# Summing chunks in four column quarters, and adding parts and base weights by matmuls, in a conditioned adapter kernel

## The chip, the cores and the metric

One core of a Trainium2 chip. The metric is the device time of one execution in microseconds (us), the median of the runs shown. Engines: TensorE (PE; PEld is its weight load), VectorE (DVE), ScalarE (ACT), GpSimd (POOL), SyncE (SP, which issues all transfers here).

## The reference

```
B, L, D, N, H = 4, 1024, 512, 128, 128
dWd = ((h @ Wdd.T + bdd) * 0.1).reshape(B, N, D)     # Wdd is (N*D, H): 32 MB
dWu = ((h @ Wdu.T + bdu) * 0.1).reshape(B, D, N)     # Wdu is (D*N, H): 32 MB
down = relu(einsum('bld,bnd->bln', x, Wd + dWd) + bd)
up   = einsum('bln,bdn->bld', down, Wu + dWu) + bu
return x + up                                        # x is (4, 1024, 512)
```

All is fp32. h is the condition, one row of 128 for each of the four batches. Four rows of h meet 131,072 rows of Wdd and Wdu, so that the work is mostly to read these two tensors and to turn their H axis onto the partitions.

## The kernel before, in words

Wdd and Wdu are read in 32 chunks each of 1 MB: a chunk is 2,048 rows, 16 on each of 128 partitions, in a ring of four buffers `w`. For each chunk VectorE transposes 32 x 32 blocks (L240, two instructions for the halves of H, `wt_front_ready` and `wt_ready`) from `w` into a ring of four buffers `wt`. H then lies in four quarters r, with 32 values of H and four row blocks q on the partitions.

TensorE sums a chunk (`sum_chunk`, L414): for each r one fp32 matmul with 512 moving columns of `wt`. The stationary operand `st` holds the values of h, placed so that chunk s of a group of four writes its own 16 output rows (q and batch) of 64; the rest of it is zero. Even r go to partitions 0 to 63 of the accumulator, odd r to 64 to 127: two tiles of 64 columns of the array, each of which holds a part of the sum. After four chunks (a group) ScalarE copies the accumulator, times 0.1, to `g_rows` (`copy_group`, L324), TensorE turns it with four transposes into `gt` (`turn_group`, L425), and VectorE adds one part and the base weights (L246), then the other part (L248), into `wd_b` or `wu_b`. `base_d` and `base_u` are Wd + 0.1 bdd and Wu + 0.1 bdu, made by VectorE and turned by TensorE, with a copy by ScalarE.

The Wdd stage (8 groups) does only this, in a loop of eight chunks. In the Wdu stage the order is written out by hand on each engine, by slots t = 0 to 31, one chunk each. TensorE: sum of the chunk; in slots with t % 4 = 1 the turn of the group before; in slots 0 to 15 eight transposes of x (`turn_x`, L458); in slots 3 to 18 a down unit (256 rows of x, L468); from slot 19 an up unit (L481) a slot, two where t % 4 = 2, for the first half of the output columns. When the last group is in, 16 up units follow for the second half. ScalarE copies x transposes (L349) and down units with relu (L357), in the order of slots and behind `copy_group`. VectorE adds up units to x (L290) two slots after TensorE's slot. GpSimd adds bu to x (L393). SyncE issues the loads of x (1 MB, slots 0, 3, 5, ... 15) between the chunks, each chunk once the transposes have freed its buffer, and the stores behind.

```
                act.wait_ge(chunk_summed, SLOTS * (g + 1))          # copy_group
...
                pe.wait_ge(g_ready, g + 1)                          # turn_group
...
                if j >= XT_RING:
                    act.wait_ge(down_summed, j - XT_RING + 1)       # copy_x
```

The last wait means: ScalarE's copies of x in slot t wait for the down unit that TensorE does at the end of slot t.

Of the kernel before, what the change touches and what calls it, by code (L numbers as in the profile page):

```python
# [25 lines left out]
FILL = SLOTS * (PART + Q * B)  # L26
FILL_STEP = PART + Q * B
# [36 lines left out]
def hyper_adapter(nc, x, cond, Wd, bd, Wu, bu, Wdd, bdd, Wdu, bdu, out):  # L64
# [10 lines left out]
    with ctx:  # L75
# [17 lines left out]
        base_d = sb("base_d", [P, C, N])  # L93
        base_u = sb("base_u", [P, D])
# [9 lines left out]
        nat = [down[:, b, 0:C, :] for b in range(B)]  # L104
        wd_nat, bdd_nat, wu_nat, bdu_nat = nat
# [18 lines left out]
        base_summed = sem("base_summed")  # L124
        base_turned = sem("base_turned")
        base_ready = sem("base_ready")
        wt_front_ready = sem("wt_front_ready")
        wt_ready = sem("wt_ready")
        chunk_summed = sem("chunk_summed")
        g_ready = sem("g_ready")  # L130
        g_turned = sem("g_turned")
        part1_added = sem("part1_added")
        group_added = sem("group_added")
# [20 lines left out]
        def _(sp):  # L154
# [9 lines left out]
            def turn(it):  # L164
                for u in range(TURN_CHUNKS):
                    c = TURN_CHUNKS * it + u
                    load_chunk(c, wdd_chunks[c], u % W_RING)
                    if u == 1 and isinstance(it, int):
                        load_base_d()

            def load_base_d():
                sp.dma_start(wd_nat, Wd.rearrange("n (c d) -> n c d", c=C)).then_inc(base_d_loaded, 16)
                sp.dma_start(bdd_nat, bdd.rearrange("(n c d) -> n c d", c=C, d=P)).then_inc(base_d_loaded, 16)  # L173

            def load_base_u():
                sp.dma_start(wu_nat, Wu.rearrange("(c d) n -> d c n", c=C)).then_inc(base_u_loaded, 16)
# [20 lines left out]
            for t in range(CHUNKS):  # L197
# [4 lines left out]
                load_chunk(CHUNKS + t, wdu_chunks[t], t % W_RING)  # L202
# [15 lines left out]
        def _(dve):  # L218
# [9 lines left out]
            for q in range(Q):  # L228
                rows = slice(QUAD * q, QUAD * (q + 1))
                place = st[rows].rearrange("p r (s z) -> p r s z", z=FILL_STEP)[:, :, :, q * B:(q + 1) * B]  # L230
                nc.vector.tensor_copy(place, h32[rows].unsqueeze(2).to_broadcast([QUAD, R, SLOTS, B])
                                      ).then_inc(st_ready, 1)
# [17 lines left out]
            def turned_parts():  # L250
                v = gt[:].rearrange("p c (a s b) -> p c a s b", s=SQ, b=B)
                return [v[:, :, a] for a in range(2)]

            def add_down_group(g):
                n = bass.ds(g * SQ, SQ)
                total = wd_b[:, :, :, n].rearrange("p c b s -> p c s b")
                base = base_d[:, :, n].unsqueeze(3).to_broadcast([P, C, SQ, B])
                add_group(g, turned_parts(), base, total)

            def add_up_group(g):  # L260
                d = slice((g - GROUPS) * D // GROUPS, (g - GROUPS + 1) * D // GROUPS)
                total = wu_b[:, :, d].rearrange("p b (s c) -> p c s b", c=C)
                base = base_u[:, d].rearrange("p (s c) -> p c s", c=C)
                add_group(g, turned_parts(), base.unsqueeze(3).to_broadcast([P, C, SQ, B]), total)

            def turn(it):
                for u in range(TURN_CHUNKS):
                    c = TURN_CHUNKS * it + u
                    transpose(c, u % W_RING, u % T_RING, 16 * (2 * it + u // W_RING + 1))
                    if u == 3 and isinstance(it, int):  # L270

                        dve.wait_ge(base_d_loaded, 16 * 2)
                        nc.vector.scalar_tensor_tensor(wd_nat, bdd_nat, DELTA_SCALE, wd_nat,
                                                       ALU.mult, ALU.add).then_inc(base_summed, 1)
                    if u == 3 and not isinstance(it, int):
                        add_down_group(2 * it - 1)
                    if u == SLOTS + 3:
                        if isinstance(it, int):
                            dve.wait_ge(base_ready, 1)
                        add_down_group(2 * it)  # L280
# [12 lines left out]
            for t in range(CHUNKS):  # L293
                c = CHUNKS + t
                transpose(c, t % W_RING, t % T_RING, 16 * (c // W_RING + 1))
                if t == 2:
                    dve.wait_ge(base_u_loaded, 16 * 4)
                    nc.vector.scalar_tensor_tensor(wu_nat, bdu_nat, DELTA_SCALE, wu_nat,
                                                   ALU.mult, ALU.add).then_inc(base_summed, 1)
                if t == 2 * SLOTS - 1:  # L300
                    dve.wait_ge(base_ready, 2)
                if t % SLOTS == 3:

                    g = c // SLOTS - 1
                    add_down_group(g) if g < GROUPS else add_up_group(g)
# [3 lines left out]
            for t in range(CHUNKS, CHUNKS + UP_LAG):  # L309
                if t == CHUNKS + UP_LAG - 1:  # L310
                    add_up_group(2 * GROUPS - 1)
# [6 lines left out]
        def _(act):  # L318
            def copy_group(g, n):

                act.wait_ge(chunk_summed, SLOTS * (g + 1))
# [5 lines left out]

            def turn(it):
                for u in range(TURN_CHUNKS):
                    if u == 1 and not isinstance(it, int):  # L330
                        copy_group(2 * it - 1, 1)
                    if u == 5 and isinstance(it, int):
                        act.wait_ge(base_turned, 1)
                        nc.scalar.activation(base_d[:], bank[0][:].rearrange("p (c n) -> p c n", c=C),  # L334
                                             ACT.Copy).then_inc(base_ready, 1)
                    if u == SLOTS + 1:
                        copy_group(2 * it, 0)
# [23 lines left out]
            for t in range(CHUNKS):  # L361
# [15 lines left out]
            copy_group(2 * GROUPS - 1, 1)  # L377

# [18 lines left out]
        def _(pe):  # L397
# [32 lines left out]
            def turn(it):  # L430
                for u in range(TURN_CHUNKS):
# [3 lines left out]
                    sum_chunk(c, s, u % T_RING, acc[n][:])  # L435
                    if u == 4 and isinstance(it, int):

                        pe.wait_ge(base_summed, 1)
                        for k in range(C):
                            last = nc.tensor.transpose(bank[0][:, k * P:(k + 1) * P], wd_nat[:, k], ident[:])  # L440
                        last.then_inc(base_turned, 1)
                    if u == 1 and not isinstance(it, int):
                        turn_group(2 * it - 1, 1)
                    if u == SLOTS + 1:
                        turn_group(2 * it, 0)
# [16 lines left out]
            def down_unit(j):  # L462
                pe.wait_ge(group_added, GROUPS)
# [8 lines left out]
            def up_unit(v):  # L472
                half, b, i0 = unit_at(v)
                pe.wait_ge(group_added, GROUPS + (half + 1) * GROUPS // 2)
# [11 lines left out]
            for t in range(CHUNKS):  # L486
# [52 lines left out]
```

## Time and profile before

| | |
|---|---|
| median of 3 runs | 245.08 us (244.66 to 245.51) |
| profiled execution, its time | 245.09 us |
| its span, first to last instruction | 243.2 us |
| mean granted TensorE clock | 0.989 |
| TensorE matmul busy | 215.1 us, 88% |
| VectorE busy | 189.4 us, 78% |
| ScalarE, GpSimd busy | 34.9 and 39.8 us |
| DMA | 85.35 MB, mean 351 GB/s |

Busy times are unions over an engine's instructions in the span; a matmul's end is modelled. Of a stretch, the view by windows gives busy time, granted clock (in parts of 2.4 GHz) and what the DMA engines moved.

### The profile page before, as it was taken

The numbers are of one execution on the slowest core, as the hardware profiler recorded it, in microseconds if no ns is written. First come the engines' busy times: TensorE is split into PE (matmuls) and PEld (weight loads), VectorE is DVE, ScalarE is ACT, GpSimd is POOL, SyncE is SP. The second block draws the span as 40 slices with busy tenths as digits, with TensorE's granted clock in tenths as the row PEclk, the third lists the DMA queues.
The fourth block names the chain that finished last, engine by engine and source line by source line (L and its number), as shares of the span: only waits on it lengthen the run. The fifth ranks groups of instructions, "written<-read, shape, count | busy, mean of one in ns | idle before, by whom it ended". The sixth has DMA issues, their size and how long they took to land.

```text
span 243.2 us, 2728 instructions
## 1 busy us (share of the span) xinstructions
PE 215.1 (88%) x972; PEld 98.0 (40%) x972; DVE 189.4 (78%) x200; ACT 34.9 (14%) x67; POOL 39.8 (16%) x23
## 2 busy tenths in 40 slices
PE   0798797878979796989999999999999999997991
PEld 0213121212212122446556655665644535354881
DVE  2799999899999994887377775295178999985782
ACT  2001000000000000412442333324110000000000
POOL 2000000000000000666444553465000000000000
PEclk9999999999999997999999999999999999999998
DMA  5999999999999999999999999949335889950897
GB/s 220 426 420 425 426 415 422 420 419 391 377 350 425 426 410 384 426 416 423 423 420 423 416 423 416 410 168 388 163 147 222 327 268 360 386 191 0 286 337 242
DMA packets 20419, 85.35 MB, mean 351 GB/s; under 512 B 1588, under 2 KB 10808, under 8 KB 11192
## 3 DMA queue, kind: packets, MB, share of 16 engines
q1 hardware_dynamic: 20408, 85.21, 88.6%
q8 instruction: 7, 0.11, 0.2%
q14 instruction: 4, 0.03, 0.0%
HBM read 76.81 MB, written 8.39 MB: 350 GB/s over the span
## 4 chain that ended last, share of the span: by engine, by line
PE 52%; DVE 19%; DMA 17%; issue 6%; ACT 2%; SPq 1%; DVEq 0%; ACTq 0%
PE acc L414 21%; DVE wt L240 17%; PE bank L481 12%; PE dn L468 12%; DMA w<-in_L_cond_Wdd_dram 11%; DMA w<-in_L_cond_Wdu_dram 6%; PE bank L458 5%; PE gt L425 2%; DVE wd_b L246 1%; ACT xt L349 1%; SPq L158 1%; ACT g_rows L324 1%; ACT down L357 0%; SPq L173 0%; DVE xs L290 0%
## 5 line engine op out<-in xcount | busy, mean ns | idle before, releaser
L240 DVE STREAM_TRANSPOSE wt<-w 128x1024 f32<-128x1024 f32 x128 | 149.2, 1214 | 25.4 <-DMA w<-in_L_cond_Wdu_dram 19.8
L414 PE MATMUL acc<-wt,st 128*64 128x512 f32 x512 | 132.1, 624 | 18.2 <-DVE wt L240 16.6
L414 PEld LDWEIGHTS acc<-wt,st 128*64 128x64 f32 x512 | 29.6, 138 | 96.0 <-DVE wt L240 60.8
L393 POOL TENSOR_TENSOR xs<-xs,bu_all 128x1024 f32<-128x1024 f32 x16 | 38.0, 2377 | 128.9 <-PE bank L458 128.9
L481 PE MATMUL bank<-wu_b,down 128*128 128x256 f32 x128 | 31.1, 388 | 1.4 <-DVE wu_b L248 1.4
L468 PE MATMUL dn<-xt,wd_b 128*128 128x256 f32 x128 | 30.5, 381 | 0.0
L481 PEld LDWEIGHTS bank<-wu_b,down 128*128 128x128 f32 x128 | 23.2, 190 | 12.3 <-issue 5.7
L290 DVE TENSOR_TENSOR xs<-bank,xs 128x512 f32<-128x512 f32 x32 | 21.7, 681 | 7.3 <-PE bank L481 7.3
L349 ACT ACTIVATE xt<-bank 128x512 f32<-128x512 f32 x32 | 17.5, 594 | 64.5 <-PE dn L468 44.0
L468 PEld LDWEIGHTS dn<-xt,wd_b 128*128 128x128 f32 x128 | 23.1, 190 | 4.1 <-issue 1.6
L324 ACT ACTIVATE g_rows<-acc 128x512 f32<-128x512 f32 x16 | 9.6, 599 | 93.2 <-PE acc L414 93.2
L458 PEld LDWEIGHTS bank<-ident,xs 128*128 128x128 f32 x128 | 14.6, 146 | 10.5 <-issue 10.5
L458 PE MATMUL bank<-ident,xs 128*128 128x128 f32 x128 | 18.0, 285 | 0.0
L246 DVE TENSOR_TENSOR wu_b<-gt,base_u 128x256 f32<-128x256 f32 x8 | 4.8, 603 | 13.4 <-PE gt L425 13.4
L425 PEld LDWEIGHTS gt<-ident,g_rows 128*128 128x128 f32 x64 | 6.8, 141 | 13.2 <-issue 8.1
L425 PE MATMUL gt<-ident,g_rows 128*128 128x128 f32 x64 | 10.5, 286 | 0.7 <-ACT g_rows L324 0.4
L357 ACT ACTIVATE down<-dn,bd_col 128x256 f32<-128x256 f32 x16 | 7.6, 477 | 8.8 <-PE dn L468 8.8
L248 DVE TENSOR_TENSOR wu_b<-gt,wu_b 128x256 f32<-128x256 f32 x8 | 4.9, 617 | 0.3
L248 DVE TENSOR_TENSOR wd_b<-gt,wd_b 128x256 f32 (+1 forms) x8 | 4.9, 612 | 0.3
L246 DVE TENSOR_TENSOR wd_b<-gt,base_d 128x256 f32 (+1 forms) x8 | 4.6, 570 | 0.0
L334 ACT ACTIVATE base_d<-bank 128x512 f32<-128x512 f32 x1 | 0.6, 599 | 19.8 <-PE bank L440 19.8
L402 PE MATMUL gt<-ident,xt 4*128 4x4 f32 x4 | 0.6, 248 | 2.9 <-DVE xt L221 2.9
(19 smaller groups left out, 9.5 us busy)
## 6 DMA issues: line engine op xcount, KB each, us to landing
w<-in_L_cond_Wdd_dram SPq DMA_DIRECT2D x32, 1024.0 KB, 7.3
w<-in_L_cond_Wdu_dram SPq DMA_DIRECT2D x32, 1024.0 KB, 10.0
xs<-in_x_dram SPq DMA_DIRECT2D x8, 1024.0 KB, 14.6
out_dram<-xs SPq DMA_DIRECT2D x4, 1024.0 KB, 7.1
out_dram<-xs SPq DMA_DIRECT2D x7, 512.0 KB, 3.9
out_dram<-xs SPq DMA_DIRECT2D x2, 256.0 KB, 3.6
down<-in_L_cond_Wd_dram SPq DMA_DIRECT2D x1, 256.0 KB, 7.1
down<-in_L_cond_bdd_dram SPq DMA_DIRECT2D x1, 256.0 KB, 7.3
```

What stands on the lines that cost most here:

```text
L240: nc.vector.transpose(wt[:, tslot, r:r + R // 2].rearrange("p r (k j) -> p k r j", j=QUAD), chunk[:, :, r:r + R // 2]).then_inc(ready, 1)
L246: nc.vector.tensor_tensor(total, parts[1], base, ALU.add).then_inc(part1_added, 1)
L248: nc.vector.tensor_tensor(total, parts[0], total, ALU.add).then_inc(group_added, 1)
L290: nc.vector.tensor_tensor(place, bank[v % BANK_RING][:].rearrange("p (i d) -> p i d", d=HALF), place, ALU.add).then_inc(unit_final, 1)
L324: nc.scalar.activation(g_rows[:, n].rearrange("p (j k) -> p j k", k=K), acc[n][:].rearrange("p (k j) -> p j k", k=K), ACT.Copy, scale=DELT ...
L349: nc.scalar.activation(xt[:, j % XT_RING, c0:c0 + BANK_C, :], bank[m % BANK_RING][:].rearrange("p (c l) -> p c l", c=BANK_C), ACT.Copy).th ...
L393: nc.gpsimd.tensor_tensor(xs[:, b, i0:i0 + UNIT_I], xs[:, b, i0:i0 + UNIT_I], bu_pair, ALU.add).then_inc(bu_added, 1)
L414: last = nc.tensor.matmul(a[PART * part:PART * (part + 1)], st[:, r, s * PART:(s + 1) * PART], wt[:, slot, r], start=s == 0 and r < 2, sto ...
L425: last = nc.tensor.transpose(gt[:, k], g_rows[:, n, k * P:(k + 1) * P], ident[:])
L458: last = nc.tensor.transpose(bank[m % BANK_RING][:, n * P:(n + 1) * P], xs[:, b, i0 + i, c * P:(c + 1) * P], ident[:])
L468: last = nc.tensor.matmul(dn[:], wd_b[:, c, j // BATCH_UNITS], xt[:, j % XT_RING, c], start=c == 0, stop=c == C - 1)
L481: last = nc.tensor.matmul(bank[v % BANK_RING][:, i * HALF:(i + 1) * HALF], down[:, b, i0 + i], wu_b[:, b, half * HALF:(half + 1) * HALF], ...
```

## The change

A chunk pair is summed at once (`sum_pair`). The matmuls of two chunks and of even and odd r go to four tiles of 32 columns of the array (`place`), and so to four quarters of the accumulator: (even r, first chunk), (even r, second), (odd r, first), (odd r, second). The chunks of a group are read in the order 0, 2, 1, 3, so that the pair's two quarters lie side by side as the lower and the upper half of one part. A chunk is transposed by one VectorE instruction. TensorE waits for both chunks of a pair before its sum, in even slots only.

The turn of a group is no longer four transposes. For each of four 128-column pieces of `g_rows`, one matmul multiplies it by `fold` (two identity halves added, 128 x 64), which turns and adds the two parts, and a second multiplies the base weights by columns of the identity, repeated for four batches, and accumulates in the same place. ScalarE copies the result to `wd_b` or `wu_b` (`store_group`), right behind `copy_group` in its order. The two VectorE additions go. `base_d` and `base_u` are loaded as they lie and are no longer turned beforehand.

```
-FILL = SLOTS * (PART + Q * B)
-FILL_STEP = PART + Q * B
+PAIR = 2
+TILE = 32
+FILL = PAIR * (TILE + Q * B)
+FILL_STEP = TILE + Q * B
+ORDER = (0, 2, 1, 3)
...
-                    load_chunk(c, wdd_chunks[c], u % W_RING)
+                    load_chunk(c, wdd_chunks[TURN_CHUNKS * it + u // SLOTS * SLOTS + ORDER[u % SLOTS]],
+                               u % W_RING)
...
-                sp.dma_start(wd_nat, Wd.rearrange("n (c d) -> n c d", c=C)).then_inc(base_d_loaded, 16)
+                sp.dma_start(base_d[:], Wd).then_inc(base_d_loaded, 16)
...
-                load_chunk(CHUNKS + t, wdu_chunks[t], t % W_RING)
+                load_chunk(CHUNKS + t, wdu_chunks[t // SLOTS * SLOTS + ORDER[t % SLOTS]], t % W_RING)
...
-            def transpose(c, slot, tslot, loaded):
+            def transpose(c, pair, slot, tslot, loaded):
                 dve.wait_ge(w_loaded[slot], loaded)
                 if later(c, T_RING):
-                    dve.wait_ge(chunk_summed, c - T_RING + 1)
-                chunk = w[:, slot, :].rearrange("p (k r h) -> p k r h", r=R, h=QUAD)
-                for r, ready in ((0, wt_front_ready), (R // 2, wt_ready)):
-                    nc.vector.transpose(wt[:, tslot, r:r + R // 2].rearrange("p r (k j) -> p k r j", j=QUAD),
-                                        chunk[:, :, r:r + R // 2]).then_inc(ready, 1)
-
-            def add_group(g, parts, base, total):
-
-                dve.wait_ge(g_turned, g + 1)
-                nc.vector.tensor_tensor(total, parts[1], base, ALU.add).then_inc(part1_added, 1)
-                dve.wait_ge(part1_added, g + 1)
-                nc.vector.tensor_tensor(total, parts[0], total, ALU.add).then_inc(group_added, 1)
...
+                    dve.wait_ge(pair_summed, pair - T_RING // PAIR + 1)
+                nc.vector.transpose(wt[:, tslot].rearrange("p r (k j) -> p k r j", j=QUAD),
+                                    w[:, slot, :].rearrange("p (k r h) -> p k r h", r=R, h=QUAD)
+                                    ).then_inc(wt_ready, 1)
...
+                        nc.vector.tensor_tensor(fold[:], ident[:, 0:PART], ident[:, PART:P], ALU.add
+                                                ).then_inc(fold_ready, 1)
...
+            def store_group(g, total):
+
+                act.wait_ge(g_turned, g + 1)
+                nc.scalar.activation(total, gt[:, :, 0:PART].rearrange("p c (s b) -> p c s b", b=B), ACT.Copy
+                                     ).then_inc(group_ready, 1)
...
                 if t % SLOTS == 1:
                     g = c // SLOTS - 1
                     copy_group(g, g % 2)
-                if t == SLOTS + 1:
-                    act.wait_ge(base_turned, 2)
-                    nc.scalar.activation(base_u[:], gt[:].rearrange("p c n -> p (c n)"), ACT.Copy
-                                         ).then_inc(base_ready, 1)
+                    down_group(g) if g < GROUPS else up_group(g)
...
-            def sum_chunk(c, s, slot, a):
-
-
-                pe.wait_ge(wt_front_ready, c + 1)
+            def sum_pair(c, low, slot, a):
+
+                pe.wait_ge(wt_ready, c + PAIR)
                 for r in range(R):
-                    if r == R // 2:
-                        pe.wait_ge(wt_ready, c + 1)
-                    part = r % 2
-                    last = nc.tensor.matmul(a[PART * part:PART * (part + 1)],
-                                            st[:, r, s * PART:(s + 1) * PART], wt[:, slot, r],
-                                            start=s == 0 and r < 2, stop=s == SLOTS - 1 and r >= 2)
-                last.then_inc(chunk_summed, 1)
-
-            def turn_group(g, n):
+                    for h in range(PAIR):
+                        place = 2 * (r % 2) + h
+                        last = nc.tensor.matmul(a[TILE * place:TILE * (place + 1)],
+                                                st[:, r, low * TILE:(low + 1) * TILE], wt[:, slot + h, r],
+                                                start=low == 0 and r < 2, stop=low == 1 and r >= 2)
+                last.then_inc(pair_summed, 1)
+
+            def turn_group(g, n, base, select):
 
                 pe.wait_ge(g_ready, g + 1)
                 if later(g, 1):
-                    pe.wait_ge(group_added, g)
+                    pe.wait_ge(group_ready, g)
                 for k in range(C):
-                    last = nc.tensor.transpose(gt[:, k], g_rows[:, n, k * P:(k + 1) * P], ident[:])
+                    nc.tensor.matmul(gt[:, k, 0:PART], g_rows[:, n, k * P:(k + 1) * P], fold[:],
+                                     start=True, stop=False)
+                    last = nc.tensor.matmul(gt[:, k, 0:PART], base(k),
+                                            select(k).unsqueeze(2).to_broadcast([P, SQ, B]),
+                                            start=False, stop=True)
                 last.then_inc(g_turned, 1)
...
-                sum_chunk(c, s, t % T_RING, acc[n][:])
+                if s % PAIR == 0:
+                    sum_pair(c, s // PAIR, t % T_RING, acc[n][:])
                 if s == 1:
                     g = c // SLOTS - 1
                     if t == SLOTS + 1:
-                        pe.wait_ge(base_ready, 2)
-                    turn_group(g, g % 2)
+                        pe.wait_ge(base_u_summed, 1)
+                    turn_down_group(g, g % 2) if g < GROUPS else turn_up_group(g)
...
-                if t == SLOTS:
-
-                    pe.wait_ge(base_summed, 2)
-                    pe.wait_ge(group_added, GROUPS)
-                    for k in range(C):
-                        last = nc.tensor.transpose(gt[:, k], wu_nat[:, k], ident[:])
-                    last.then_inc(base_turned, 1)
-            turn_group(2 * GROUPS - 1, 1)
+            turn_up_group(2 * GROUPS - 1)
```

## Rows read from the trace of the kernel before

**Rows 1.** The page: the chain that ended last, share of the span by engine.
```profile
PE 52%; DVE 19%; DMA 17%; issue 6%; ACT 2%; SPq 1%; DVEq 0%; ACTq 0%
```

**Rows 2.** Windows by stage: length, busy us (instructions) by engine, PEclk, DMA share, GB/s.
```profile
15.00:90.00 75.00, 64.75 (x266) 15.42 (x264) 73.86 (x72) 4.67 (x8) 0.00 (x0) 1.00 1.00 410
90.00:110.65 20.65, 16.80 (x82) 7.83 (x80) 14.08 (x15) 3.85 (x7) 8.97 (x4) 0.92 1.03 407
110.65:168.77 58.12, 57.41 (x307) 34.85 (x308) 38.65 (x36) 19.34 (x40) 28.35 (x13) 1.00 0.95 391
...
183.47:224.16 40.69, 39.34 (x172) 17.84 (x172) 36.56 (x44) 1.79 (x3) 0.00 (x0) 1.00 0.70 250
```

**Rows 3.** The same view, ten undisturbed us of the Wdd stage.
```profile
80.00:90.00 10.00, 8.61 (x38) 2.09 (x36) 10.00 (x10) 0.60 (x1) 0.00 (x0) 1.00 1.01 424
```

**Rows 4.** The chain in order of time (start us, us, what), slots 6 to 10.
```profile
121.11 1.87 PE acc L414 x8
122.97 1.03 PE bank L458 x8
...
134.98 0.02 issue
...
137.06 0.66 PE gt L425 x4
137.71 0.87 PE bank L458 x8
138.59 1.73 PE dn L468 x8
140.32 1.87 PE acc L414 x8
```

**Rows 5.** The same view, slots 20 to 31 and the last block.
```profile
183.47 1.87 PE acc L414 x8
...
189.72 1.87 PE acc L414 x8
...
202.69 1.87 PE acc L414 x8
...
224.16 14.09 PE bank L481 x64
```

**Rows 6.** Timeline of TensorE's weight loads, slot 9.
```profile
135.38 0.14 PEld L414 LDWEIGHTS acc<-wt,st 128*64 128x64 f32 x2 [0.28 <-issue]
135.81 0.14 PEld L414 LDWEIGHTS acc<-wt,st 128*64 128x64 f32 x2 [0.28 <-issue]
137.06 0.42 PEld L425 LDWEIGHTS gt<-ident,g_rows 128*128 128x128 f32 x4 [1.10 <-ACT g_rows L324]
```

**Rows 7.** Groups of instructions: xcount | busy us, mean ns | idle before.
```profile
L414 PEld LDWEIGHTS acc<-wt,st 128*64 128x64 f32 x512 | 29.6, 138 | 96.0 <-DVE wt L240 60.8 <-issue 33.4 <-ACT g_rows L324 1.0
L468 PEld LDWEIGHTS dn<-xt,wd_b 128*128 128x128 f32 x128 | 23.1, 190 | 4.1 <-issue 1.6
L425 PE MATMUL gt<-ident,g_rows 128*128 128x128 f32 x64 | 10.5, 286 | 0.7 <-ACT g_rows L324 0.4 <-ACT base_u L368 0.3
L357 ACT ACTIVATE down<-dn,bd_col 128x256 f32<-128x256 f32 x16 | 7.6, 477 | 8.8 <-PE dn L468 8.8
```

**Rows 8.** Timeline of VectorE at four places.
```profile
83.81 5.71 DVE L240 STREAM_TRANSPOSE wt<-w 128x1024 f32<-128x1024 f32 x5
...
111.85 4.86 DVE L240 STREAM_TRANSPOSE wt<-w 128x1024 f32<-128x1024 f32 x4 [1.66 <-DMA w<-in_L_cond_Wdu_dram]
...
193.43 1.25 DVE L290 TENSOR_TENSOR xs<-bank,xs 128x512 f32<-128x512 f32 x2
...
225.40 0.69 DVE L290 TENSOR_TENSOR xs<-bank,xs 128x512 f32<-128x512 f32 x1 [0.70 <-PE bank L481]
```

**Rows 9.** Timeline of TensorE at the start of the Wdu stage.
```profile
93.35 3.01 PE L414 MATMUL acc<-wt,st 128*64 128x512 f32 x8 [2.69 <-DVE wt L240]
...
98.24 2.21 PE L414 MATMUL acc<-wt,st 128*64 128x512 f32 x8 [0.17 <-DVE wt L240]
```

More of the change, by code:

```diff
@@ L92, in hyper_adapter @@
         xt = sb("xt", [P, XT_RING, C, UNIT_I * P])
-        base_d = sb("base_d", [P, C, N])
-        base_u = sb("base_u", [P, D])
+        base_d = sb("base_d", [P, D])
+        base_u = sb("base_u", [P, C, N])
+        fold = sb("fold", [P, PART])
         st = sb("st", [P, R, FILL])
@@ L102, in hyper_adapter @@
         cond_rep = xt[0:B, 0, 1:3, :].rearrange("b c (r q i) -> b (c r) q i", q=Q, i=QUAD)
-        nat = [down[:, b, 0:C, :] for b in range(B)]
-        wd_nat, bdd_nat, wu_nat, bdu_nat = nat
+        bdd_nat = down[:, 0, 0:C, :].rearrange("p c n -> p (c n)")
+        bdu_nat = down[:, 1, 0:C, :]
         acc = [pb(f"acc{n}", [P, COLS]) for n in range(2)]
@@ L250, in turned_parts @@
[L250 to L264, printed above, removed]
+                    dve.wait_ge(pair_summed, pair - T_RING // PAIR + 1)
@@ L268, in turn @@
                     c = TURN_CHUNKS * it + u
-                    transpose(c, u % W_RING, u % T_RING, 16 * (2 * it + u // W_RING + 1))
+                    transpose(c, SLOTS * it + u // PAIR, u % W_RING, u % T_RING, 16 * (2 * it + u // W_RING + 1))
                     if u == 3 and isinstance(it, int):
+                        dve.wait_ge(ident_ready, 1)
+                        nc.vector.tensor_tensor(fold[:], ident[:, 0:PART], ident[:, PART:P], ALU.add
+                                                ).then_inc(fold_ready, 1)
                         dve.wait_ge(base_d_loaded, 16 * 2)
[L273 to L280, printed above, removed]
+                        nc.vector.scalar_tensor_tensor(base_d[:], bdd_nat, DELTA_SCALE, base_d[:],
+                                                       ALU.mult, ALU.add).then_inc(base_d_summed, 1)
             turn(0)
@@ L326, in copy_group, with down_group, up_group @@
                                      ACT.Copy, scale=DELTA_SCALE).then_inc(g_ready, 1)
-            def turn(it):
[L329 to L337, printed above, removed]
+            def store_group(g, total):
+                act.wait_ge(g_turned, g + 1)
+                nc.scalar.activation(total, gt[:, :, 0:PART].rearrange("p c (s b) -> p c s b", b=B), ACT.Copy
+                                     ).then_inc(group_ready, 1)
+            def down_group(g):
+                store_group(g, wd_b[:, :, :, bass.ds(g * SQ, SQ)].rearrange("p c b s -> p c s b"))
+            def up_group(g):
+                d = slice((g - GROUPS) * D // GROUPS, (g - GROUPS + 1) * D // GROUPS)
+                store_group(g, wu_b[:, :, d].rearrange("p b (s c) -> p c s b", c=C))
+            def turn(it):
+                for n in range(2):
+                    if n == 1 or not isinstance(it, int):
+                        copy_group(2 * it + n - 1, 1 - n)
+                        down_group(2 * it + n - 1)
             turn(0)
@@ new lines, in turn_group, with turn_down_group, turn_up_group @@
+                    last = nc.tensor.matmul(gt[:, k, 0:PART], base(k),
+                                            select(k).unsqueeze(2).to_broadcast([P, SQ, B]),
+                                            start=False, stop=True)
+                last.then_inc(g_turned, 1)
+            def turn_down_group(g, n):
+                turn_group(g, n, lambda k: base_d[:, k * P:(k + 1) * P],
+                           lambda k: ident[:, bass.ds(g * SQ, SQ)])
+            def turn_up_group(g):
+                first = (g - GROUPS) * D // GROUPS
+                row = first % P
+                pick = ident[:, row:row + D // GROUPS].rearrange("p (s c) -> p c s", c=C)
+                turn_group(g, g % 2, lambda k: base_u[:, first // P], lambda k: pick[:, k])
@@ L434, in turn @@
                         pe.wait_ge(g_ready, 2 * it + n - 1)
-                    sum_chunk(c, s, u % T_RING, acc[n][:])
-                    if u == 4 and isinstance(it, int):
-                        pe.wait_ge(base_summed, 1)
-                        for k in range(C):
-                            last = nc.tensor.transpose(bank[0][:, k * P:(k + 1) * P], wd_nat[:, k], ident[:])
-                        last.then_inc(base_turned, 1)
+                    if s % PAIR == 0:
+                        sum_pair(c, s // PAIR, u % T_RING, acc[n][:])
                     if u == 1 and not isinstance(it, int):
-                        turn_group(2 * it - 1, 1)
+                        turn_down_group(2 * it - 1, 1)
                     if u == SLOTS + 1:
-                        turn_group(2 * it, 0)
+                        if isinstance(it, int):
+                            pe.wait_ge(fold_ready, 1)
+                            pe.wait_ge(base_d_summed, 1)
+                        turn_down_group(2 * it, 0)
             turn(0)
@@ L473, in up_unit @@
                 half, b, i0 = unit_at(v)
-                pe.wait_ge(group_added, GROUPS + (half + 1) * GROUPS // 2)
+                pe.wait_ge(group_ready, GROUPS + (half + 1) * GROUPS // 2)
                 pe.wait_ge(down_ready, (b * I + i0 + UP_I) // UNIT_I)
```

39 lines of the change are left out of this document (15 added, 24 removed).

## The prediction

> **What bounds the kernel now.** I read the chain of waits first. TensorE holds 52% of it, VectorE 19%, DMA 17% [rows 1]. The table by stages [rows 2] tells where each of them bounds. From 15 to 90 us, the Wdd stage, VectorE is busy 73.9 of 75 us and DMA moves 410 GB/s, where an undisturbed stretch of it shows 424 [rows 3]. Both are near their limit there; TensorE only waits for chunks. From 90 to 110.65 chunks come late, because x shares the DMA. From 110.65 to 224.16 TensorE is hardly ever free (57.4 of 58.1 and 39.3 of 40.7 us), and the last 14.1 us of up matmuls are its own too. So a change is worth what it does to TensorE's own order of work from slot 4 of the Wdu stage on (slot t is the pass of the loop that handles Wdu chunk t).
>
> The chain in order of time gives the price of each piece [rows 4]: a chunk's sum 1.87 us, the eight x transposes 1.02 behind a sum and 0.87 behind a turn (so leaving the narrow-column mode costs 0.15), a down unit 1.73. Four slots, 8 to 12 by pattern, go from 121.11 to 140.32 (slots 6 to 10): 19.21 us. In the up stage four slots take 202.69 - 189.72 = 12.97 us [rows 5].
>
> **The sums.** Before, a chunk's sum issues its later loads two at a time, at 135.38 and 135.81 [rows 6]: two 64-column tiles side by side, a step of 0.43 us each, four steps and 0.15 to leave: 1.87. After, a pair of chunks is summed with four 32-column tiles. If four streams run side by side as two do now, it is again four steps: S = 1.87 us for two chunks, 0.94 for one. Fewest: the same 1.87, since each stream still has 512 columns. Most: only two at a time, eight steps, S = 3.59. I take 1.87, because two streams cost nothing over one in the row. In a sentence that nothing here needs: the Trainium skill, "TensorE: Matmul & The Clock Gate", section "Measured speedup vs the span model", has three column tiles at 2.38 times one, not 3; no row here runs more than two tiles, and by 2.38 of 3 a step would be about 0.54, S 2.3, and the time about 246.
>
> **The turns.** Four transposes of one load each become eight fp32 matmuls, which this trace records as two load-and-matmul pairs each (512 load records for 256 sum matmuls, 64 matmul records for the 64 transposes [rows 7]): 16 pairs. The old four loads take 0.42 us from 137.06, a start every 0.11 [rows 4, 6]. A load of 128 fp32 columns takes 190 ns, one of 64 138 [rows 7]: 52 ns for 64 columns, so 0.107 for 128. The moving side has now 64 columns, 0.053. If the next load runs under the matmul, a pair takes 0.109 and the turn T = 16 x 0.109 + 0.1 = 1.85 us; if they are serial, 0.16 a pair and 2.66; if only the moving side counted, 0.97. I take 1.85, since the later loads of a sum lie wholly under its matmuls [rows 6]. Before, it was 0.44 to 0.66. So T gives back 1.2 to 1.4 us for each group, against two sums (3.74) saved.
>
> **A cover that goes.** A turn stands in slots with t % 4 = 1 and waits for ScalarE's copy of the group. Ahead of that copy ScalarE has two copies of x, which wait for the down unit of the slot before, and copy_down. From the end of that down unit (134.98) to the turn (137.06) are 2.08 us [rows 4]. Now the slot's own sum lies under this; after the change an odd slot has no sum, and TensorE stands still for 2.08 us. In slot 17 no x copy is left in front; I estimate that half of it, 1.0, remains. From slot 21 on ScalarE is idle and the copy is done early. ScalarE's new wait, for the turn, has the slot's x copies and copy_down queued behind it; these need the down unit at the end of that slot anyway, so nobody waits for them longer.
>
> **Four slots of the x and down stage, after:** two sums 3.74, x transposes 1.02 + 0.87 + 1.02 + 0.87 = 3.78, down units 6.92, T 1.85, the wait 2.08: 18.37 us against 19.21.
>
> **Wdd stage and start.** The two additions go from VectorE. A half transpose starts every 1.13 us by the merged rows [rows 8], so a chunk costs 2.25 and now at most that (one instruction of 2,048 instead of two: I take 2.2); a chunk's bytes take 2.47 at 424 GB/s. DMA alone bounds then: 75 x (424 - 410)/424 = 2.5 us earlier at 90. Slot 4 now waits for chunk 5 as well, transposed today at 111.85 + 2.3 = 114.2; less 2.5 it is 111.7, and slot 4 starts at 111.8 instead of 110.65. The lost microsecond is repaid at once: 4.62 + (2.08 + 1.85 + 0.87 + 1.73) + 4.62 + 2.60 (slots 4 to 7, the last without a sum and a switch of mode) brings slot 8 to 130.2. Two blocks of 18.37: slot 16 at 166.9. Slots 16 to 19: 1.87 + 1.88; 1.0 + 1.85 + 1.73; 1.87 + 1.88; one up unit 0.87: 12.95, so slot 20 at 179.9 against 183.47 [rows 5]. The base additions, the base transposes and ScalarE's base copies that go, the small addition for fold, the straight loads of Wd and Wu and the new order of chunks (the same bytes in the same number of transfers), lie beside chunks that are waited for; 0.5 us at slot 5 is in the sum.
>
> **The up stage.** VectorE works in order: transpose, additions of two slots back, transpose. The pair's sum now needs the second chunk's whole transpose, which stands behind the addition of a unit that TensorE finished only after the pair before. So the pair's period is: S 1.87, up unit to its addition 1.24 (224.16 to 225.40), addition 0.58 (two in 1.25) [rows 5, 8], transpose 2.2, 0.1 for the semaphore: 5.99; with two units in the even slot 0.87 more, about 6.85. TensorE alone would need 1.87 + 0.87 + T + 0.87 + 0.1 = 5.56. Four slots: 12.84 against 12.97; nearly all of the saving there is lost to this loop. Pairs from 20 to 29: 3 x 5.99 + 2 x 6.85 = 31.7, so slot 30 at 211.6. Then sum and three units 4.63, T 1.85, 0.2 of latency, ScalarE's copy 0.48 (its 256-column copy has 477 ns [rows 7]) and 0.1: the last up block starts at 218.8 against 224.16. Behind it nothing changes: 5.3 us saved.
>
> **Sum.** Profiled time 245.09 (span 243.2, 1.9 around it; the median of the runs is 245.08): 245.1 - 5.3 = 239.8 us.
>
> **Rivals.**
> *Four streams don't run side by side (slower).* Place: the 14 pair sums from slot 4. Each 0.1 us more in S costs 1.4 us; from S = 2.25 on the gain is gone, at two at a time (3.59) it is 14 x 1.72 = 24 us: 264. For it: four moving streams are nowhere in the trace. Against: two run at full speed. Chance 0.14, half of it between.
> *The turn is dearer.* At T = 2.66: 0.81 more in slots 5, 9, 13, 17 and in the last turn (4.05), and what is over 0.3 of slack in 21, 25, 29 (1.4): 245.3, no change. Chance 0.12.
> *The clock falls.* After 2.69 us of idling TensorE ran a sum in 3.01 instead of 2.2 us, granted clock 0.92 over that stretch [rows 2, 9]; that is time at 1.2 instead of 2.4 GHz. After the change, TensorE idles about 3 us in every pair period of 4.95 in the Wdd stage. Were it at 1.2 GHz there, a pair costs 3.6 and a turn up to 3.6: two pairs and a turn 10.8 against 9.9 us of DMA, at worst 0.9 x 7 = 6 us; at the least the first slots of the next stage cost 2 us more. I take 3: 243. Of this the Trainium skill speaks too ("TensorE: Matmul & The Clock Gate", "HAM oscillation — how this bites in real kernels"): bursts of matmuls with DMA waits between start each at half clock. The trace shows it once. Chance 0.13.
> *It does nothing*, because chunks or VectorE bind all of 110 to 224: against it, DMA moves only 250 GB/s from 183 us on [rows 2], and TensorE is busy 39.3 of 40.7 us there. Chance 0.06, between 244 and 246.
>
> **How the numbers follow.** The sum as worked has 0.55, own range 236 (T at its lower end) to 243.5. With the rivals the range is 236 to 248.5; what is left out is mostly the far half of the first rival and a still faster turn. Within 0.3% (0.7 us) is what this kernel's runs can't tell from no change. Faster: 0.55 + most of the clock's 0.13 + 0.02 = 0.67; same 0.10; slower 0.23.
>
> **What would show it.** Sum of a pair: four load groups 0.43 apart, 1.87 start to start. Turn: 16 pairs 0.11 apart. A TensorE wait of about 2.1 us for the ScalarE copy in slots 5, 9, 13, about 1 in 17. Slot 20 near 180, the last up block at 219. VectorE's share near 70%, at 10 to 90 us DMA at 424 GB/s without dips. The prediction is wrong if the pair's steps are longer than 0.43, the turn over 2.6, or the granted clock of the Wdd stage well under 1.

## The result, and the profile after

The changed kernel takes 253.21 us (median of 4 runs, 252.28 to 255.34) where the one before takes 245.24: a ratio of 1.034, 95% interval 1.026 to 1.042 (behind later ratios it stands in brackets). It is slower by 8 us; 239.8 was forecast, and the range ended at 248.5. The profiled execution has 252.29 us and a span of 250.5.

The page of the changed kernel, busy time and instructions by engine, and the chain by engine:

```profile
PE 192.9 (77%) x1156; PEld 116.3 (46%) x1156; DVE 170.4 (68%) x105; ACT 43.7 (17%) x81; POOL 38.7 (15%) x23
...
PEclk9999965779798755999799889959999999999998
...
PE 41%; DMA 31%; DVE 16%; issue 5%; ACT 3%; SPq 1%; DVEq 0%; ACTq 0%
```

TensorE has 22 us less to do than before, VectorE 19 less, and DMA's share of the chain went from 17% to 31%: in the Wdd stage it is the bound now, at 419 GB/s, with VectorE busy 67 of 75 us. The row to stop at is PEclk. Its mean is 0.886, where it was 0.989.

By stage, windows of the changed kernel, cut at the starts of slots 4, 8, 12, 16, 20 and 30 (columns as in rows 2):

```profile
15.00:90.00 75.00, 57.30 (x340) 24.89 (x344) 67.26 (x31) 8.58 (x14) 0.00 (x0) 0.80 1.01 419
90.00:113.30 23.30, 15.77 (x108) 8.19 (x101) 14.44 (x7) 5.17 (x11) 8.24 (x4) 0.76 1.02 416
113.30:134.50 21.20, 18.25 (x112) 13.23 (x112) 12.88 (x6) 6.03 (x13) 10.60 (x5) 0.92 1.01 421
134.50:155.70 21.20, 18.30 (x113) 13.43 (x112) 10.12 (x5) 6.91 (x14) 9.42 (x4) 0.92 0.92 374
155.70:178.60 22.90, 20.00 (x116) 14.79 (x115) 9.01 (x4) 6.91 (x14) 9.42 (x4) 0.85 0.50 183
178.60:191.80 13.20, 12.15 (x77) 7.67 (x76) 4.50 (x2) 4.23 (x9) 0.00 (x0) 1.00 0.63 250
191.80:224.00 32.20, 26.36 (x177) 16.32 (x176) 30.02 (x23) 3.35 (x6) 0.00 (x0) 1.00 0.73 272
```

The Wdd stage moves 419 GB/s (410 before, rows 2). Four slots of the x and down stage take 21.2, 21.2 and 22.9 us; 18.4 was forecast and 19.2 is what they took before [rows 4]. TensorE is busy 18.3 of 21.2 us in the first two and, worse, not at full speed: the granted clock is 0.92 and 0.85 in windows where it was 1.00 [rows 2]. From slot 20 to slot 30 it is 32.2 us.

What one such block looks like, the chain in order of time from the down unit of slot 7 on:

```profile
131.52 0.59 ACT xt L326
132.12 0.37 ACT down L334
132.49 0.14 issue
132.62 1.97 PE dn L453 x8
134.59 1.85 PE acc L387 x16
136.44 1.02 PE bank L443 x8
137.46 1.74 PE dn L453 x8
139.25 0.04 issue
...
141.28 0.43 PE gt L398 x2
141.71 0.22 PE gt L400 x2
141.94 0.22 PE gt L398 x2
142.16 0.22 PE gt L400 x2
142.38 0.35 PE gt L398 x2
142.73 0.43 PE gt L400 x2
...
144.01 1.71 PE bank L443 x8
145.72 1.81 PE dn L453 x8
```

Three things are to be seen. A pair's sum takes 1.85 us for two chunks, as forecast. TensorE stands still from 139.20 to 141.28 for ScalarE's copy, as forecast. But in the middle of the turn two load-and-matmul pairs go from 0.22 us to 0.43, and the eight x transposes behind it take 1.71 instead of 0.87: TensorE has gone from 2.4 to 1.2 GHz. The granted clock (the column before the last two, 1.00 for 2.4 GHz) before and behind that point, and behind the wait of slot 13:

```profile
139.00:142.40 3.40, 1.31 (x11) 1.12 (x10) 1.77 (x1) 1.94 (x4) 0.90 (x1) 0.99 1.01 422
142.40:145.70 3.30, 3.30 (x17) 3.30 (x17) 0.54 (x1) 0.63 (x1) 0.00 (x0) 0.50 1.02 422
...
163.00:169.60 6.60, 6.60 (x28) 6.15 (x28) 0.00 (x0) 0.63 (x1) 1.94 (x1) 0.50 0.61 240
```

The same follows the waits of slots 5 and 13, each time a wait of about 2.1 us and then the turn: 3.4, 3.4 and 6.8 us at half speed in slots 5, 9 and 13, 13.7 in all (from the clocks of the windows above). Behind the shorter wait of slot 17 (1.05 us) the clock stays.

A wait of this length doesn't always bring the fall. In the up stage TensorE idles 2.30 us before the sums of slots 24 and 28, and the clock is 1.00 behind both:

```profile
204.91 1.92 PE L387 MATMUL acc<-wt,st 128*32 128x512 f32 x16 [2.30 <-DVE wt L243]
217.98 1.92 PE L387 MATMUL acc<-wt,st 128*32 128x512 f32 x16 [2.30 <-DVE wt L243]
```

The first lines of the chain show a wait that I had not seen at all: the down unit of slot 7 waits for ScalarE's copy of the one before. That wait in the changed kernel (in total, times, longest, us):

```profile
PE dn L453 <- ACT down L334: 2.5, 3, 0.8
```

### The profile page after: what moved, and what is told of

It reads as the page before. It is cut to its first block, busy times and chain, and to the rows that moved or that the text cites. A ratio compares the mean times of both kernels' runs of the same rounds, so it can differ in the third digit from the quotient of the medians.

```text
span 250.5 us, 3007 instructions
## 1 busy us (share of the span) xinstructions
PE 192.9 (77%) x1156; PEld 116.3 (46%) x1156; DVE 170.4 (68%) x105; ACT 43.7 (17%) x81; POOL 38.7 (15%) x23
## 4 chain that ended last, share of the span: by engine, by line
PE 41%; DMA 31%; DVE 16%; issue 5%; ACT 3%; SPq 1%; DVEq 0%; ACTq 0%
DMA w<-in_L_cond_Wdd_dram 23%; DVE wt L243 16%; PE dn L453 12%; PE acc L387 11%; PE bank L466 9%; DMA w<-in_L_cond_Wdu_dram 8%; PE bank L443 4%; PE gt L398 2%; PE gt L400 2%; ACT xt L326 1%; ACT down L334 1%; SPq L162 1%; ACT g_rows L293 1%; DVE xs L267 0%; SPq L178 0%
## 5 line engine op out<-in xcount | busy, mean ns | idle before, releaser
L243 DVE STREAM_TRANSPOSE wt<-w 128x2048 f32<-128x2048 f32 x64 | 147.2, 2306 | 55.5 <-PE acc L387 25.7
L387 PE MATMUL acc<-wt,st 128*32 128x512 f32 x512 | 78.3, 739 | 38.0 <-DVE wt L243 38.0
L387 PEld LDWEIGHTS acc<-wt,st 128*32 128x32 f32 x512 | 15.4, 122 | 79.9 <-issue 49.0
L398 PE MATMUL gt<-fold,g_rows 128*128 128x64 f32 x128 | 29.3, 317 | 8.6 <-ACT g_rows L293 6.5
L398 PEld LDWEIGHTS gt<-fold,g_rows 128*128 128x128 f32 x128 | 23.6, 228 | 21.9 <-issue 13.8
L400 PE MATMUL gt<-ident,base_d 128*128 (+1 forms) x64 | 14.9, 322 | 0.0
L300 ACT ACTIVATE wd_b<-gt 128x256 f32 (+1 forms) x8 | 5.1, 639 | 53.8 <-PE gt L400 53.8
L400 PE MATMUL gt<-ident,base_u 128*128 128x64 f32 x64 | 13.8, 302 | 0.0
L400 PEld LDWEIGHTS gt<-ident,base_d 128*128 128x128 f32 x64 | 12.3, 239 | 0.0
L400 PEld LDWEIGHTS gt<-ident,base_u 128*128 128x128 f32 x64 | 11.1, 216 | 0.0
```

Source lines behind the costliest of these rows:

```text
L243: nc.vector.transpose(wt[:, tslot].rearrange("p r (k j) -> p k r j", j=QUAD), w[:, slot, :].rearrange("p (k r h) -> p k r h", r=R, h=QUAD) ...
L300: nc.scalar.activation(total, gt[:, :, 0:PART].rearrange("p c (s b) -> p c s b", b=B), ACT.Copy).then_inc(group_ready, 1)
L387: last = nc.tensor.matmul(a[TILE * place:TILE * (place + 1)], st[:, r, low * TILE:(low + 1) * TILE], wt[:, slot + h, r], start=low == 0 an ...
L398: nc.tensor.matmul(gt[:, k, 0:PART], g_rows[:, n, k * P:(k + 1) * P], fold[:], start=True, stop=False)
L400: last = nc.tensor.matmul(gt[:, k, 0:PART], base(k), select(k).unsqueeze(2).to_broadcast([P, SQ, B]), start=False, stop=True)
```

## The experiments

All are timed against runs of the kernel before on the same chip (244.85 to 245.09 us).

Theory: the pair sums took away the work under which TensorE's waits for ScalarE lay, and such a wait costs twice, once as idle time and once as time at 1.2 GHz behind it. Rivals: the turn's 16 pairs are what costs; or the clock falls because TensorE has too little to do, wherever its waits are.

**The turn alone.** The changed kernel with `sum_chunk`, the two wide tiles and the half transposes of before:

```
-            def sum_pair(c, low, slot, a):
+            def sum_chunk(c, s, slot, a):
...
-                    sum_pair(c, s // PAIR, t % T_RING, acc[n][:])
+                sum_chunk(c, s, t % T_RING, acc[n][:])
```

> The changed kernel with the sums of before: one chunk at a time, two tiles of 64 columns, two half transposes; only the turn by 16 load-and-matmul pairs and ScalarE's store are left of the change. Theory of the uncovered wait (the slowdown comes from odd slots that lost their sum, and from the clock that falls after the wait): the wait of 2.1 us is gone, the granted clock is 0.98 as before, and the time is that of before plus the dearer turn, about 1.3 us in each of slots 5, 9, 13, 17, 21, 25, 29 and 0.7 in the last: 254 less 1 to 2 us for the Wdd stage, so 252 to 254. Rival, the turn is nearly free (it hides) and everything lost is the pair's: 246. Rival, the turn's small matmuls themselves make the clock fall: granted clock under 0.92 here too, and over 255.

Measured: 253.84 us, ratio 1.040 (1.033 to 1.047). The clock is 0.989. Its windows for slots 8 to 11 and 20 to 29:

```profile
130.20:150.70 20.50, 20.28 (x113) 12.78 (x112) 12.49 (x12) 6.92 (x14) 9.39 (x5) 1.00 1.01 421
...
187.40:223.80 36.40, 36.40 (x179) 18.53 (x178) 30.79 (x32) 3.10 (x5) 0.00 (x0) 1.00 0.73 256
```

A turn costs 1.3 us more than before in each block and 1.4 in the up stage, as worked out, and with TensorE busy all the time the clock never falls, dear turn or not. So the turn is a loss of some 9 us on its own, and the pair sums have to earn it back. The rival that the turn is nearly free falls, and so does the one that its small matmuls alone make the clock fall.

**The sums alone.** The kernel before with `sum_pair`, one transpose a chunk, and its old turn and additions:

```
-                sum_chunk(c, s, t % T_RING, acc[n][:])
+                if s % PAIR == 0:
+                    sum_pair(c, s // PAIR, t % T_RING, acc[n][:])
```

> The kernel before with the pair sums (four tiles, one transpose a chunk, even slots only), and the old turn with four transposes and VectorE's two additions. Theory of the uncovered wait: odd slots wait for ScalarE still, 2.1 us in slots 5, 9, 13 and 0.8 for the down copy in slots 7, 11, 15, and the clock falls after them (granted clock under 0.95): four slots take 18 to 21 us and the time is 241 to 247. Rival, the turn is what was lost: the clock stays and four slots take 17 us: 235 to 238.

Measured: 246.76 us (four runs from 243.35 to 248.71), ratio 1.010 (1.005 to 1.016). The profile is of the fastest of these, so that its times are a lower end. Slots 8 to 11 and 12 to 15:

```profile
132.40:152.30 19.90, 17.00 (x101) 11.66 (x101) 12.58 (x7) 6.28 (x13) 9.45 (x4) 0.91 1.01 421
152.30:170.50 18.20, 15.30 (x101) 10.44 (x100) 10.04 (x6) 6.28 (x13) 9.45 (x4) 1.00 0.63 244
```

Halving TensorE's largest piece of work made the kernel no faster. The waits are there (2.9 us of 18.2 idle). The clock falls behind the wait of slot 9, for 3.4 us, but not behind those of slots 5 and 13, which are as long:

```profile
139.17 0.66 PE L424 MATMUL gt<-ident,g_rows 128*128 128x128 f32 x4 [2.09 <-ACT g_rows L325]
...
159.06 0.66 PE L424 MATMUL gt<-ident,g_rows 128*128 128x128 f32 x4 [2.09 <-ACT g_rows L325]
```

So the waits came as expected and the falls in one case of three. The time is near the theory's upper end (247), with runs so far apart that a few us can't be argued from it. The rival that only the turn is dear falls: this kernel has the cheap turn, and 235 to 238 was its forecast. In the up stage it waits 2.8 us before the sums of slots 24 and 28, also without a fall.

**The turn where it is covered.** The changed kernel; the turns of slots 5, 9, 13, 17 stand in slots 7, 11, 15, 19, between the x transposes and the down unit, and ScalarE's store with them:

```
+TURN_AT = {1: 7, 7: 8, 11: 9, 15: 10, 19: 11, 21: 12, 25: 13, 29: 14}
...
-                if s == 1:
-                    g = c // SLOTS - 1
+                if t in TURN_AT:                 # behind turn_x
+                    g = TURN_AT[t]
```

> The changed kernel with the turns of slots 5, 9, 13, 17 two slots later (7, 11, 15, 19), behind the x transposes and ahead of the down unit, and ScalarE's store with them; nothing else is moved. Theory of the uncovered wait: TensorE has no wait for a group's copy, the one for the down copy in slots 7, 11, 15 lies under the turn, four slots take 16.5 to 17.5 us, the granted clock from slot 4 on is 1: 239 to 243. Rival, the clock falls because TensorE has too little to do anyway, not because of this wait: only the waits go, and the time is 246 to 249 with the clock still at 0.90. Rival, the turn's price is what matters: 252.

Measured: 240.87 us, ratio 0.983 (0.979 to 0.986). Slots 8 to 11:

```profile
130.50:147.80 17.30, 16.48 (x117) 11.91 (x119) 9.24 (x4) 6.93 (x14) 9.47 (x4) 1.00 1.01 421
```

The same instructions in another order are 12.3 us faster, and 1.7% faster than the kernel before. The clock is 1.00 in all of slots 4 to 19, though the Wdd stage has the same mean of 0.80: little to do in that stage is not what made it fall later. In the up stage this kernel's clock fell once, behind one of its two waits of 2.30 us, and that stage took 33.8 us instead of 32.2:

```profile
191.84 2.99 PE L390 MATMUL acc<-wt,st 128*32 128x512 f32 x16 [2.30 <-DVE wt L244]
```

**The wait filled.** The changed kernel with useless matmuls in the waits of slots 5, 9, 13 (four) and 17 (two); nothing else moves:

```
+                    for _ in range(fill):
+                        nc.tensor.matmul(gt[:, 0:2, :].rearrange("p c n -> p (c n)"), ident[:],
+                                         wd_b[:, 0, 0:2, :].rearrange("p b n -> p (b n)"), start=True, stop=True)
                 pe.wait_ge(g_ready, g + 1)
```

> The changed kernel with four useless fp32 matmuls of 256 columns (two in slot 17) where TensorE waits for ScalarE's copy in slots 5, 9, 13 and 17; they write to gt ahead of the turn, which starts it anew. The waits stay as long. Theory that the clock falls because of the idle stretch: it stays at 1 from slot 4 on, and up to half of the 13.7 us at the lower clock in that stretch comes back: 247 to 249. Rival, the clock falls for another reason (small matmuls of the turn, or little to do in the Wdd stage): 252 to 254, low stretches where they were.

Measured: 245.08 us, ratio 1.002 (0.999 to 1.005). The window of slots 4 to 19:

```profile
113.20:185.20 72.00, 68.27 (x444) 48.49 (x448) 36.63 (x16) 24.41 (x50) 29.71 (x13) 1.00 0.84 341
```

And the timeline of TensorE's matmuls in slot 9, from the filling to the turn:

```profile
137.29 1.89 PE L398 MATMUL gt<-wd_b,ident 128*128 128x256 f32 x8
139.54 0.43 PE L404 MATMUL gt<-fold,g_rows 128*128 128x64 f32 x2 [0.36 <-ACT g_rows L294]
139.81 0.39 PE L406 MATMUL gt<-ident,base_u 128*128 128x64 f32 x2
```

The turn starts 2.2 us after the down unit (2.1 without the filling), no sooner, and work was only added; yet the clock is 1.00 throughout and 16 slots take 72.0 us instead of 78.6. 6.6 us is about half of 13.7: the clock's whole price in the profiled run. The medians differ by 8.1 us, more than expected. In the profiled runs the spans differ by 7.8: 6.6 in these slots, and 1.1 behind the start of the last up block, where TensorE's own matmuls take the same 14.1 us, so that this part is not the clock's. The runs of the changed kernel had mean clocks of 0.87 to 0.91, those with the filling 0.90 to 0.93.

So in slots 5, 9 and 13 the idle stretch is what the fall needs: with it filled the profile has none, with the turn moved away from it there is none (the run before), and the turn alone without a wait has none. It is not enough by itself. The up stage's waits of 2.30 us, two in each of five profiles (changed, turns covered, wait filled, down copy first, Wdd stage kept busy), brought a fall once in ten, and waits of 2.1 us with a turn of four transposes behind them once in three. What else decides it, the 16 small pairs behind the wait or the work ahead of it, no run here separates.

**The down copy first.** The kernel with covered turns, and in ScalarE's order of a slot:

```
+                if t in DOWN_AT:
+                    copy_down(DOWN_AT[t])
                 if t < X_BANKS // 2:
                     copy_x(2 * t)
                     copy_x(2 * t + 1)
-                if t in DOWN_AT:
-                    copy_down(DOWN_AT[t])
```

> The kernel with covered turns, and ScalarE copies a down unit ahead of the slot's two copies of x instead of behind them. The wait of 0.82 us before the down unit of slots 5, 9, 13 and 17, which my prediction left out, is gone if it is this order that makes it: four slots 16.5 us instead of 17.3, 2 to 3 us in all, 238 to 239. Rival, the down unit waits for its x copies, or the copies of x now come late for the x transposes: no change, 240.9.

Measured: 237.95 us, ratio 0.970 (0.966 to 0.975). The waits (in total, times, longest), first of the kernel with covered turns:

```profile
PE dn L456 <- ACT down L335: 3.1, 4, 0.8
```

and of the one with the down copy first, whose slots 8 to 11 take 16.2 us:

```profile
PE dn L456 <- ACT down L335: 0.7, 1, 0.7
```

Three of four waits are gone; in the 16.2 us TensorE is busy all the time (window 132.40 to 148.60). In this run's profile TensorE waited 2.95 us for the chunk of slot 4, and that slot's sum ran at half clock and took 3.25 us, not 1.92.

**Additions three slots behind**, on that kernel and on the changed one: `UP_LAG = 3` instead of 2.

> The same, with VectorE's additions of up units three slots behind TensorE instead of two. Theory that in the up stage the pair's sum waits for an addition that waits for the pair before: TensorE's wait there goes, four slots take 12.1 us (VectorE: 4 transposes of 2.31 and 5 additions of 0.58) instead of 12.8 to 14.7, and the clock has no reason to fall there: 235 to 237. Rival, VectorE is the bound of the stage whatever the order: within 0.7 us of the run before it.

> The changed kernel with the additions three slots behind, and nothing else. By the same theory 1.5 to 2.5 us faster than the changed kernel: 250.5 to 252; by the rival 253.

Measured: 230.88 us, ratio 0.943 (0.939 to 0.946), and 247.70 us, ratio 1.010 (1.006 to 1.015). Both gain more than I expected, 7.1 and 5.5 us where 1 to 3 and 1.5 to 2.5 were forecast. The first kernel's windows for slots 8 to 11 and 20 to 29:

```profile
129.90:146.10 16.20, 16.20 (x117) 11.84 (x116) 10.43 (x5) 6.93 (x14) 9.47 (x4) 1.00 1.01 420
...
176.10:203.10 27.00, 26.08 (x179) 16.20 (x178) 26.71 (x21) 3.10 (x5) 0.00 (x0) 1.00 0.78 290
```

The ten slots take 27.0 us instead of 32.2, and now TensorE (26.1 busy) and VectorE (26.7) are both nearly always busy in them. The changed kernel with the lag takes 27.0 us for them too, 5.2 less than without, and the rival (VectorE bounds the stage whatever the order) falls. I had expected VectorE's work by count, 12.1 us for four slots; it starts the stage ahead, so that less of it falls within (21 of its instructions against 23). The gain in ten slots is 5.2 us of the 7.1; in the profiled runs the rest is the late and slow sum of slot 4 in the kernel that it is compared with, ahead of anything that the lag touches.

**The Wdd stage kept busy.** The changed kernel, and later the fastest one, with two useless matmuls behind each pair's sum in the loop of the Wdd stage:

```
+                        if not isinstance(it, int):
+                            for _ in range(2):
+                                nc.tensor.matmul(bank[0][:], ident[:], base_d[:], start=True, stop=True)
```

> The changed kernel with two useless fp32 matmuls of 512 columns behind each pair's sum in the loop of the Wdd stage (identity by base weights, into a bank that is free then). Theory that the lower clock of that stage is hidden by DMA and that only the slots from 5 on cost: granted clock of the Wdd stage near 1, slot 4 starts at 112 to 113, the time is 251 to 253, with the low stretches of slots 5 to 17 where they were. Rival, my prediction's own: the clock in the Wdd stage costs 3 us or more: 248 to 250. Rival, the clock once held up stays up to the end: 246.

> The run with covered turns, down copy first and lag 3, with the two useless matmuls behind each pair's sum in the loop of the Wdd stage. Theory that the low clock of the Wdd stage is hidden behind DMA: slot 4 starts at 113 as before, time within 1 us of 230.9. Rival: it costs some us even there, and the time is 228 to 229.

Measured: 251.84 us, ratio 1.030 (1.025 to 1.035); and 230.43 us, ratio 0.941 (0.940 to 0.942). The changed kernel with it, Wdd stage, slots 0 to 3, slots 4 to 19:

```profile
15.00:90.00 75.00, 66.31 (x396) 28.04 (x396) 67.22 (x31) 8.73 (x14) 0.00 (x0) 0.98 1.01 418
90.00:113.30 23.30, 15.13 (x101) 8.44 (x94) 14.44 (x7) 5.35 (x11) 8.50 (x4) 0.93 1.03 416
113.30:191.90 78.60, 68.79 (x414) 49.06 (x414) 36.51 (x16) 23.90 (x49) 29.20 (x13) 0.91 0.78 311
```

The clock of the Wdd stage rises from 0.80 to 0.98, and neither DMA's rate nor the start of slot 4 (113.3) changes, nor do the 78.6 us behind it. The intervals overlap with those of the unfilled kernels in both cases. What TensorE loses in the Wdd stage is hidden behind DMA, as far as these runs can tell: the fastest kernel's two intervals leave room for 1.6 us at most, not for the rival's. The slow sum of slot 4 in one profile (the down copy first, above) is a case where it came through.

**Control: the same moves on the kernel before**, down copy first and `UP_LAG = 3`:

> The kernel before, with ScalarE's down copy ahead of its x copies and VectorE's additions three slots behind: the two moves that brought the changed kernel from 240.9 to 230.9. Theory that they only mend waits that pair sums bring: TensorE has no such wait in the kernel before, so the time is 244 to 245.5. Rival, the moves are worth something by themselves and the change is worth less than it seems: 240 or less.

Measured: 244.66 us, ratio 0.999 (0.998 to 1.001). The moves are worth nothing in the kernel before; they mend waits that pair sums bring. (The third move, a turn with cover, this kernel has already.) The gain of the 230.88 us kernel is that of the change, once its waits are covered.

## Why the prediction was wrong

The chip's times against the steps of the prediction, profiled executions, us from the span's start:

| | forecast | changed kernel | wait filled | covered, down first, lag 3 |
|---|---|---|---|---|
| slot 4 starts | 111.8 | 113.3 | 113.2 | 113.5 |
| slots 4 to 19 | 68.1 | 78.6 | 72.0 | 62.6 |
| slots 20 to 29 | 31.7 | 32.2 | 32.1 | 27.0 |
| slot 30 to the last block | 7.2 | 7.2 | 7.2 | |

- **The sums**: right. The later loads of a sum stand 0.43 us apart, four at a time (below), and a pair takes 1.85. Four tiles run side by side as two did. The Trainium skill ("TensorE: Matmul & The Clock Gate", "Measured speedup vs the span model") has three column tiles at 2.38 times one; steps of 0.54, my estimate from that figure, are not what this trace shows for four.

```profile
134.97 0.13 PEld L387 LDWEIGHTS acc<-wt,st 128*32 128x32 f32 x4 [0.30 <-issue]
135.40 0.13 PEld L387 LDWEIGHTS acc<-wt,st 128*32 128x32 f32 x4 [0.30 <-issue]
```

- **The turns**: right in the size, two pairs in 0.22 us, T = 1.8 without a wait and 2.0 behind one, and +1.3 us for each when alone. One of its two sources was luck: I got 0.107 us for a load of 128 columns from 190 and 138 ns, but the old turn's own loads of 128 columns have 141 ns in the page of before. What carried it was the start every 0.11 us.

```profile
L425 PEld LDWEIGHTS gt<-ident,g_rows 128*128 128x128 f32 x64 | 6.8, 141 | 13.2 <-issue 8.1
```

The slack between 5.99 and 5.56 is 0.43 us, not the 0.3 that the rival of the dearer turn used: it would have come to 245.0, not 245.3.
- **The cover that goes**: this is the step that failed. The wait was found, with its size, 2.08 us, but only its idle time was charged. In slots 5, 9 and 13 the clock fell behind it, which cost 6.6 us (78.6 less 72.0). I had the clock's fall as a rival but placed it in the Wdd stage, where TensorE idles longer and where it does happen, and where it costs nothing measurable (the stage kept busy: slot 4 no earlier). My sign of being wrong, the clock of the Wdd stage well under 1, did come, and pointed to the wrong stage. In the stage where I counted TensorE's microseconds one by one I took them all at 2.4 GHz.
- **Four slots of the x and down stage**: 18.37 forecast, 19.6 with the wait filled. 0.82 of the 1.2 us is the wait for the down copy in the other odd slot, for which I had the rows (two x copies ahead of it in ScalarE's order) and asked only for the turn, not for the next instruction that waits for ScalarE. 2.5 us in three slots; putting the down copy first, on the kernel with covered turns, gave 2.9. The rest, 0.4 us a block, is in the chain of the kernel with the wait filled: behind a wait a turn takes 2.00 us and a down unit 1.97, where 1.85 and 1.73 were forecast.
- **Wdd stage and start**: DMA moved 419 GB/s in the Wdd stage, not 424, which by the prediction's own sum is 0.9 us; slot 4 started 1.5 us late (1.4 to 1.7 in the three kernels of the table), behind the transpose of chunk 5, which ended at 113.1 and not at 111.7. The other 0.6 us I can't place.
- **The up stage**: right, 32.2 us for ten slots against 31.7, with VectorE's transpose behind an addition that waits for the pair before, and it was this loop that ate the gain: before, the same ten slots took 32.2 too (183.47 to 215.66). That it could be opened by one slot of lag, for 5.5 us, the prediction did not ask.
- **The sum**: 218.8 forecast for the last block, 231.2 measured: 1.5 at the start, 6.6 by the clock, 3.9 by the waits for the down copy and the slower starts behind waits in slots 4 to 19, 0.4 behind.

The clock's price of 3 us was too small for want of asking where in the kernel it would not be hidden. The Trainium skill ("TensorE: Matmul & The Clock Gate", "HAM oscillation — how this bites in real kernels") tells of bursts of matmuls that start at half clock behind waits for DMA. The trace agrees in part: in the Wdd stage, where TensorE waits for chunks, the mean is 0.80, full and half clock by turns; behind waits of 2.1 us for ScalarE in slots 5, 9 and 13 the clock fell each time, and behind those of 2.30 us in the up stage mostly not.

## What to carry to other kernels

When an engine's work is made shorter, list every wait that lay under it, and every instruction on that engine that waits for the same partner, not only the first. Price an idle stretch of TensorE as the stretch and, as a chance where TensorE is the bound behind it, some microseconds at half clock too (0 to 6.8 behind each wait of 2 us here); a few useless matmuls in the wait tell in one run which of the two it is. A change that frees an engine can be a loss until the order written for the old durations is redone: here the same work in another order went from 253.2 to 230.9 us, while the same moves did nothing for the old kernel.

## What the runs showed of the hardware

Four fp32 matmuls of 128 x 32 by 512 columns run side by side in four column tiles with a step of 0.43 us, the same as two of 64. The load-and-matmul pairs of the turn (64 moving columns, a new stationary operand of 128 columns each) go at 0.11 us a piece; those of the x transposes, with 128 moving columns, go at 0.11 us too (eight in 0.87), so that the moving columns are not what sets the pace of the turn's pairs. One transpose of 2,048 elements on each partition takes 2.31 us on VectorE against 2.25 for two halves by their starts. And of waits and turns together, in slots 4 to 19:

| | waits of 2.1 us | turn | at 1.2 GHz, profiled run |
|---|---|---|---|
| before | none | 4 transposes | 0 |
| turn alone | none | 16 pairs | 0 |
| sums alone | three | 4 transposes | 3.4 us, behind one |
| changed | three | 16 pairs | 13.7 us, behind all three |
| changed, wait filled | filled | 16 pairs | 0 |
| changed, turns covered | none | 16 pairs | 0 |
